# A two-layer graph network with pre-norm on one core: where the last rounds' aggregates stand, who scales two norms, and the first batch of the W2 stage

## The chip, the cores and the metric

The kernel runs on one core of a Trainium2 chip. Its time is the device time in microseconds (us) of one execution. The engines are PE (TensorE; PEld is its weight load), DVE (VectorE), ACT (ScalarE), POOL (GpSimd) and SP (SyncE, which here only issues DMAs); each runs its own queue in order, and semaphores join them.

## What is computed

The input is x (16 batches, 512 tokens, 128 features) and an adjacency matrix. Two residual blocks follow, each on relu(layernorm(x)).

```python
h = relu(layernorm(x)); x = x + L0(h, adj)
h = relu(layernorm(x)); x = x + L1(h, adj)

# L0: two graph layers, then LSTMs over windows of 1 to 4 tokens
h = relu(einsum('ts,bsh->bth', adj, x @ Wg0 + bg0))
h = relu(einsum('ts,bsh->bth', adj, h @ Wg1 + bg1))
for p in (1, 2, 3, 4):
    last = lstm_last(Wih[p-1], Whh[p-1], ..., windows of p tokens)
    h = h.at[:, last token of each window].set(last)

# L1: normalised adjacency, two linear layers, two batch norms over all tokens
A_hat = A_norm * dinv[:, None] * dinv[None, :]
agg = einsum('nm,bmd->bnd', A_hat, features)
h = relu(batchnorm(agg @ W1.T + b1, g1, be1))     # 256 features
out = batchnorm(h @ W2.T + b2, g2, be2)           # 128 features
```

A batch norm needs the statistics of all 16 batches, so it is a barrier between stages.

## The kernel before, in words

Every float32 product is made of three matmuls with operands split in a high and a low part (`product`, lines 1020 to 1022): ACT writes the high part (`..._hi`), DVE the low part (`..._lo`, `low`, lines 712 and 714).

The 16 batches go through the LSTM in four rounds of four batches, two chains of two batches each. A round has 22 turns (`ORDER`), 11 for each chain; the whole has 88 (`N_SLOTS`). In each turn every engine runs its `lstm_turn`. Behind a turn come pieces of other stages: `PRE_AFTER` and `POST_AFTER` are lists by turn, filled from the positions in `PRE_POS` and `POST_POS`. The pieces of L1 for a batch n below 12 (`LATE`) come one round after its LSTM: "turn" (PE transposes the batch's states, DVE adds them to x1, line 812), "stats" (DVE's statistics, lines 758 and 761), "norm" (POOL computes the layer norm: lines 347 and 348, the power at 350, four scalings of 128x128 at 353; then ACT's nrm_hi, line 571, and DVE's nrm_lo), "agg" (12 matmuls of 512 columns into post_ps; ACT's agg_hi, line 597; DVE's agg_lo) and "hid0" and "hid1" (W1, three matmuls each; ACT writes z, line 592; DVE takes its statistics, line 820). For batch 11 the aggregate stands behind turn 85, W1's halves behind 86 and 87, which are the last two turns. A position is the place in each engine's queue; nothing is reordered at run time.

Behind the last turn each engine has its own hand-written list for batches 12 to 15. PE: four groups of transposes, alternately into pre_ps and post_ps, then aggregates and W1 halves, each aggregate one batch ahead of its W1. POOL: the four norms in order, into `y_last`. DVE and ACT: as PE's list needs them.

Then comes the first batch norm (`batch_norm`, DVE lines 962 to 974, POOL's power at 393). The W2 stage goes over the batches in `END_ORDER`, 8 to 11 first, the spilled 0 to 7, then 12 to 15. For the k-th of them, z's two halves of 128x512 are scaled and shifted in place; who does it is fixed by `DVE_HALVES` (line 988), `ACT_HALVES` (679) and `POOL_HALVES`, which are all others (406). Then ACT makes hid_hi (693, both halves at once, 128x1024), DVE hid_lo (712), PE the six matmuls of W2, ACT takes them out (671) and DVE takes the statistics (993). The second batch norm is built by the same functions, and the last stage scales (703, 414), transposes (1238), adds x1 (1012) and stores.

SP loads z_back back from memory once the graph layers of all batches are done, and x1_back (3 MB) once the LSTM is.

## Time and profile before

| | |
|---|---|
| median of 3 runs | 585.74 us |
| lowest and highest | 584.45 and 585.82 us |
| the profiled execution, its own time | 586.14 us |
| its span | 584.3 us |
| busy: PE, DVE, ACT, POOL | 517.1, 426.0, 358.1, 203.1 us |
| last LSTM turns and their moved pieces | 485.0 to 494.9 us |
| transposes, norms, aggregates and W1 of batches 12 to 15 | 494.9 to 524.6 us |
| first batch norm | 524.6 to 527.3 us |
| W2 stage | 527.3 to 566.3 us |
| second batch norm and last stage | 566.3 to 584.3 us |

Times in views are us from the start of the span. A timeline row gives start, duration, engine, line, operation, output<-input and forms; in brackets it has the idle time of the engine before it and the instruction that ended it. A duration is longer than the time to the next start where instructions overlap in the engine's pipeline. PEclk is TensorE's granted clock as a share of full speed.

### The profile page before, as it was taken

What the parts mean: (1) busy time and instruction counts of PE and PEld (TensorE: products, weight loads), DVE (VectorE), ACT (ScalarE), POOL (GpSimd) and SP (SyncE); (2) the same over time, 40 slices, a digit from 0 to 9 for tenths busy, and PEclk for the clock granted to TensorE, in tenths of its full rate; (3) what the DMA queues carried; (4) which work ended last, traced back from release to release, by engine and by line L of the source; (5) the groups of instructions that cost most, each with busy time, mean ns of one, the idle gap of its engine ahead of it and who ended that gap; (6) DMA issues with size and microseconds to landing.
All of it is one profiled execution on the core that took longest, in us unless ns stands there. A gap on an engine that the chain in (4) does not pass through costs nothing.

```text
span 584.3 us, 8178 instructions
## 1 busy us (share of the span) xinstructions
PE 517.1 (88%) x2769; PEld 443.8 (76%) x2769; DVE 426.0 (73%) x968; ACT 358.1 (61%) x680; POOL 203.1 (35%) x310
## 2 busy tenths in 40 slices
PE   4998998798899999999999999998699989685856
PEld 3787687798887789899877898997487978464536
DVE  3656757878867888687688886856767876666876
ACT  2545755556468567575776675756647766157854
POOL 5402021304400854163008442510233241709941
PEclk9999999798999999999999999999989989796998
DMA  8300020000001111010110210105510000500007
GB/s 232 94 19 2 0 91 19 2 17 2 19 18 56 37 72 52 22 48 27 54 74 19 72 55 1 55 2 186 211 36 1 20 18 2 216 0 1 1 0 289
DMA packets 17838, 31.22 MB, mean 53 GB/s; under 512 B 1498, under 2 KB 6020, under 8 KB 17796
## 3 DMA queue, kind: packets, MB, share of 16 engines
q1 hardware_dynamic: 16804, 30.17, 14.9%
q10 hardware_dynamic: 992, 0.52, 0.4%
q8 instruction: 22, 0.36, 0.3%
q14 instruction: 20, 0.16, 0.1%
HBM read 19.16 MB, written 11.53 MB: 53 GB/s over the span
## 4 chain that ended last, share of the span: by engine, by line
PE 50%; issue 18%; DVE 13%; POOL 9%; ACT 6%; POOLq 2%; DMA 1%; DVEq 0%; ACTq 0%
PE gate_ps L1020 10%; PE gate_ps L1021 10%; PE gate_ps L1022 10%; POOL z_back L406 4%; PE pre_ps L1021 4%; PE pre_ps L1022 4%; PE pre_ps L1020 4%; PE post_ps L1020 2%; POOL x_pre L353 2%; PE post_ps L1022 2%; PE post_ps L1021 2%; ACT gate L626 2%; POOLq L351 2%; ACT gate L616 1%; DVE cell L894 1%
## 5 line engine op out<-in xcount | busy, mean ns | idle before, releaser
L616 ACT ACTIVATE gate<-gate_ps,gate_bias 128x256 f32<-128x256 f32 (+2 forms) x312 | 164.8, 564 | 48.0 <-PE gate_ps L1022 46.4
L1020 PE MATMUL gate_ps<-by_class_hi,wih_hi 128*128 128x256 f32 (+2 forms) x264 | 86.5, 328 | 12.5 <-POOL by_class_lo L372 6.8
L626 ACT ACTIVATE gate<-cell 128x512 f32<-128x512 f32 (+2 forms) x88 | 45.3, 515 | 69.1 <-DVE cell L889 35.7
L1022 PE MATMUL gate_ps<-by_class_lo,wih_hi 128*128 128x256 f32 (+2 forms) x264 | 84.9, 322 | 0.0
L1021 PE MATMUL gate_ps<-by_class_hi,wih_lo 128*128 128x256 f32 (+2 forms) x264 | 84.9, 321 | 0.0
L1020 PEld LDWEIGHTS gate_ps<-by_class_hi,wih_hi 128*128 128x128 f32 x264 | 51.2, 194 | 19.6 <-POOL by_class_lo L372 7.5
L1020 PE MATMUL gate_ps<-hstep_hi,whh_hi 128*128 128x256 f32 (+2 forms) x192 | 61.2, 319 | 0.0
L1021 PE MATMUL gate_ps<-hstep_hi,whh_lo 128*128 128x256 f32 (+2 forms) x192 | 61.2, 319 | 0.0
L1022 PE MATMUL gate_ps<-hstep_lo,whh_hi 128*128 128x256 f32 (+2 forms) x192 | 61.0, 318 | 0.0
L372 POOL TENSOR_TENSOR by_class_lo<-h,by_class_hi 128x256 fp32r<-128x256 f32 (+1 forms) x40 | 35.4, 891 | 61.0 <-ACT by_class_hi L624 61.0
L347 POOL TENSOR_TENSOR ln_pre<-mv_pre,eps 128x4 f32<-128x4 f32 x16 | 5.0, 316 | 143.0 <-DVE mv_pre L761 143.0
L1021 PEld LDWEIGHTS gate_ps<-by_class_hi,wih_lo 128*128 128x128 f32 x264 | 51.1, 193 | 3.7
L1022 PEld LDWEIGHTS gate_ps<-by_class_lo,wih_hi 128*128 128x128 f32 x264 | 51.0, 193 | 2.3
L347 POOL TENSOR_TENSOR ln_post<-mv_post,eps 128x4 f32<-128x4 f32 x16 | 6.1, 383 | 132.5 <-DVE mv_post L761 132.5
L899 DVE TENSOR_TENSOR gate<-gate 128x256 f32<-128x256 f32 (+2 forms) x48 | 26.8, 558 | 26.4 <-ACT gate L626 26.4
L1022 PEld LDWEIGHTS gate_ps<-hstep_lo,whh_hi 128*128 128x128 f32 x192 | 37.5, 195 | 1.4
L1021 PEld LDWEIGHTS gate_ps<-hstep_hi,whh_lo 128*128 128x128 f32 x192 | 37.5, 195 | 1.3
L1020 PEld LDWEIGHTS gate_ps<-hstep_hi,whh_hi 128*128 128x128 f32 x192 | 37.5, 195 | 1.3
L353 POOL TENSOR_SCALAR x_pre<-x_pre,ln_pre 128x128 f32<-128x128 f32 x64 | 34.8, 558 | 2.8 <-issue 2.8
L353 POOL TENSOR_SCALAR y_post<-x,ln_post 128x128 f32<-128x128 f32 x56 | 34.8, 636 | 2.5 <-issue 2.5
L886 DVE TENSOR_TENSOR gate<-gate 128x256 f32<-128x256 f32 (+2 forms) x48 | 24.2, 504 | 15.1 <-ACT gate L616 15.0
L889 DVE TENSOR_TENSOR cell<-cell,gate 128x256 f32<-128x256 f32 (+2 forms) x48 | 25.5, 532 | 5.0
(285 smaller groups left out, 1393.9 us busy)
## 6 DMA issues: line engine op xcount, KB each, us to landing
x_pre<-in_x SPq DMA_DIRECT2D x16, 256.0 KB, 2.7
x<-in_x SPq DMA_DIRECT2D x16, 256.0 KB, 2.7
z_spill<-z_ring SPq DMA_DIRECT2D x8, 512.0 KB, 2.8
z_back<-z_spill SPq DMA_DIRECT2D x8, 512.0 KB, 7.2
x_spill<-x SPq DMA_DIRECT2D x12, 256.0 KB, 2.2
x_back<-x_spill SPq DMA_DIRECT2D x1, 3072.0 KB, 11.1
out<-x_back SPq DMA_DIRECT2D x12, 256.0 KB, 2.3
x<-in_adj SPq DMA_DIRECT2D x1, 1024.0 KB, 6.3
```

The source lines that it names most:

```text
L351: nc.gpsimd.drain()
L353: last = nc.gpsimd.tensor_scalar(y[:, c * P:(c + 1) * P], src[:, c * P:(c + 1) * P], ln[:, 2, c:c + 1], ln[:, 1, c:c + 1], ALU.add, ALU.mult)
L372: nc.gpsimd.tensor_tensor(lo, states, f32(hi), ALU.subtract).then_inc(later_lo, 1)
L406: nc.gpsimd.tensor_scalar(zz, zz, bn1[:, 4, half:half + 1], bn1[:, 5, half:half + 1], ALU.mult, ALU.add).then_inc(t_pool, 1)
L616: nc.scalar.activation(gate[:, tile_of(g), gt, 0:size], gate_ps[k % GATE_BANKS][:, 0:size], ACT.Tanh if gt == G_GATE else ACT.Sigmoid, bia ...
L626: nc.scalar.activation(gate[:, tile_of(g), G_GATE, 0:size], cell[:, tile_of(g), 0:size], ACT.Tanh)\
L886: nc.vector.tensor_tensor(i_, i_, g_, ALU.mult).then_inc(ig_done, 1)
L889: nc.vector.tensor_tensor(c_, c_, i_, ALU.add).then_inc(cell_ready, 1)
L899: nc.vector.tensor_tensor(i_, o_, g_, ALU.mult).then_inc(h_done, 1)
L1020: nc.tensor.matmul(ps, w[0], m[0], start=start, stop=False)
L1021: nc.tensor.matmul(ps, w[1], m[0], start=False, stop=False)
L1022: return nc.tensor.matmul(ps, w[0], m[1], start=False, stop=stop)
```

## The change

Four things change.

The aggregate and W1 of batch 11 (`LEFT`) leave `POST_AFTER`. They now stand in the hand-written lists: the aggregate between the second and third group of transposes, W1 behind the fourth. The tables `TURN_PS`, `AGG_PS` and `HID_PS` say which PSUM bank each group of transposes, aggregate and W1 half uses, and the lists are written out anew.

For batches 12 and 13 POOL computes only the norm's scale (`norm_scale`), and DVE does the four scalings (`tail_y_of`); batches 14 and 15 stay with POOL.

In `batch_norm` DVE negates the mean while POOL computes the power, and the last two dependent instructions become one for each group.

In the W2 stage DVE scales both halves of the first batch, and ACT scales half (1, 1) in place of (0, 1), so POOL has 24 halves in place of 25. For the first batch hid_hi and hid_lo are made half by half, and PE starts with the first half.

```diff
--- before.py
+++ after.py
@@ -89,8 +89,8 @@
-DVE_HALVES = ((0, 0),)
-ACT_HALVES = ((0, 1), (3, 1), (5, 1), (8, 1), (11, 1), (14, 1))
+DVE_HALVES = ((0, 0), (0, 1))
+ACT_HALVES = ((1, 1), (3, 1), (5, 1), (8, 1), (11, 1), (14, 1))
 POOL_HALVES = tuple((k, half) for k in range(BATCHES) for half in range(HALVES)
@@ -114,8 +114,9 @@
               if len(ORDER) * (n // PER_ROUND - 1) + spots[n % PER_ROUND] == slot] for slot in range(N_SLOTS)]
+LEFT = LATE - 1
 POST_AFTER = [[(kind, n) for kind, spots in POST_POS.items() for n in range(LATE)
-               if len(ORDER) * (n // PER_ROUND + 1) + spots[n % PER_ROUND] == slot] for slot in range(N_SLOTS)]
+               if (n < LEFT or kind in ("turn", "stats", "norm")) and len(ORDER) * (n // PER_ROUND + 1) + spots[n % PER_ROUND] == slot] for slot in range(N_SLOTS)]
@@ -199,7 +200,7 @@
         cell = sb("cell", [P, CHAINS, T], F32, main)
-        y_last = [y_post, cell[:, 0, :]]
+        y_last = [y_post[:, :], cell[:, 0, :]]
         main.close()
@@ -224,6 +225,11 @@
         post_ps = whole.enter_context(nc.psum_tensor("post_ps", [P, T], F32))
+        TURN_PS = {LATE: pre_ps, LATE + 1: post_ps, LATE + 2: gate_ps[1], LATE + 3: gate_ps[2]}
+        AGG_PS = {LEFT: gate_ps[0], LATE: gate_ps[5], LATE + 1: pre_ps, LATE + 2: post_ps, LATE + 3: gate_ps[5]}
+        HID_PS = {LEFT: (gate_ps[3], gate_ps[4]), LATE: (gate_ps[0], gate_ps[1]), LATE + 1: (gate_ps[2], gate_ps[3]),
+                  LATE + 2: (gate_ps[4], pre_ps), LATE + 3: (gate_ps[0], gate_ps[1])}
@@ -254,6 +260,7 @@
         turn_mm, x1_ready = sem("turn_mm"), sem("x1_ready")
+        tail_rstd, tail_y = sem("tail_rstd"), sem("tail_y")
         post_stats, post_y, post_nhi, post_nlo = (sem(f"post_{n}") for n in ("stats", "y", "nhi", "nlo"))
@@ -340,14 +347,18 @@
-            def layer_norm(n, y, src, mv, ln, stats, ready):
+            def norm_scale(n, mv, ln, stats):
...
                 nc.gpsimd.drain()
-                nc.gpsimd.tensor_tensor(ln[:, 1, :], ln[:, 0, :], minus_half[:, :], ALU.pow)
+                return nc.gpsimd.tensor_tensor(ln[:, 1, :], ln[:, 0, :], minus_half[:, :], ALU.pow)
+            def layer_norm(n, y, src, mv, ln, stats, ready):
+                norm_scale(n, mv, ln, stats)
                 nc.gpsimd.drain()
@@ -386,7 +397,9 @@
-            for n in range(LATE, BATCHES):
+            for n in range(LATE, LATE + 2):
+                norm_scale(n, mv_post[n % 2], ln_post[n % 2], post_stats).then_inc(tail_rstd, 1)
+            for n in range(LATE + 2, BATCHES):
                 norm_post(n, y_last[n % 2])
@@ -566,8 +579,8 @@
-            def normed(n, y, dst, ready, done):
-                act.wait_ge(ready, n + 1)
+            def normed(n, y, dst, ready, done, count=None):
+                act.wait_ge(ready, n + 1 if count is None else count)
                 nc.scalar.activation(dst[0][:, :, :].rearrange("p c d -> p (c d)"), y, ACT.Relu).then_inc(done, 1)
@@ -655,16 +668,30 @@
-            for n in range(LATE, LATE + 2):
-                normed(n, y_last[n % 2][:, :], nrm[n % 2], post_y, post_nhi)
-            for n in range(LATE, BATCHES + 1):
-                if n < BATCHES:
-                    agg_out(n, gate_ps[n % 2], n % 2)
-                if n + 2 < BATCHES:
-                    normed(n + 2, y_last[n % 2][:, :], nrm[n % 2], post_y, post_nhi)
-                if n > LATE:
-                    for half in range(HALVES):
-                        hid_out(n - 1, half, gate_ps[2 + 2 * ((n - 1) % 2) + half])
+            def tail_norm(n):
+                if n < LATE + 2:
+                    normed(n, y_last[n % 2], nrm[n % 2], tail_y, post_nhi, n - LATE + 1)
+                else:
+                    normed(n, y_last[n % 2], nrm[n % 2], post_y, post_nhi, n - 1)
+            def tail_hid(n):
+                for half in range(HALVES):
+                    hid_out(n, half, HID_PS[n][half])
+            agg_out(LEFT, AGG_PS[LEFT], 1)
+            tail_norm(LATE)
+            tail_hid(LEFT)
+            tail_norm(LATE + 1)
+            agg_out(LATE, AGG_PS[LATE], 0)
+            tail_norm(LATE + 2)
+            agg_out(LATE + 1, AGG_PS[LATE + 1], 1)
+            tail_hid(LATE)
+            tail_norm(LATE + 3)
+            agg_out(LATE + 2, AGG_PS[LATE + 2], 0)
+            tail_hid(LATE + 1)
+            agg_out(LATE + 3, AGG_PS[LATE + 3], 1)
+            tail_hid(LATE + 2)
+            tail_hid(LATE + 3)
@@ -682,12 +709,17 @@
                 for j, half in ACT_HALVES:
-                    if j == (k + 1 if k else 0):
+                    if j == k + 1:
                         hid_t(j, half)
-                act.wait_ge(t_dve, halves_to(DVE_HALVES, k))
+                if k == 0:
+                    for half in range(HALVES):
+                        act.wait_ge(t_dve, half + 1)
+                        nc.scalar.activation(hid[0][0][:, half, :], z_end(b)[:, half * T:(half + 1) * T], ACT.Relu)\
+                            .then_inc(hid_hi, 1)
+                    continue
                 act.wait_ge(t_act, halves_to(ACT_HALVES, k))
-                if k > 0:
-                    act.wait_ge(t_pool, halves_to(POOL_HALVES, k))
+                act.wait_ge(t_pool, halves_to(POOL_HALVES, k))
                 if k >= 3:
@@ -943,21 +975,46 @@
-            for n in range(LATE, BATCHES):
-                turned(n, (pre_ps, post_ps)[n % 2])
-                if n < LATE + 2:
-                    stats_post(n)
-            for n in range(LATE, LATE + 2):
-                normed(n, y_last[n % 2][:, :], nrm[n % 2], post_nhi, post_nlo)
-                stats_post(n + 2)
-            for n in range(LATE, BATCHES + 1):
-                if n < BATCHES:
-                    agg_out(n, gate_ps[n % 2], n % 2)
-                if n + 2 < BATCHES:
-                    normed(n + 2, y_last[n % 2][:, :], nrm[n % 2], post_nhi, post_nlo)
-                if n > LATE:
-                    for half in range(HALVES):
-                        hid_stats(n - 1, half)
+            def tail_y_of(n):
+                dve.wait_ge(tail_rstd, n - LATE + 1)
+                for c in range(CHUNKS):
+                    last = nc.vector.tensor_scalar(y_last[n % 2][:, c * P:(c + 1) * P],
+                                                   x1[:, n % PER_ROUND, c * P:(c + 1) * P], ln_post[n % 2][:, 2, c:c + 1],
+                                                   ln_post[n % 2][:, 1, c:c + 1], ALU.add, ALU.mult)
+                last.then_inc(tail_y, 1)
+            def tail_norm(n):
+                normed(n, y_last[n % 2], nrm[n % 2], post_nhi, post_nlo)
+            def tail_hid(n):
+                for half in range(HALVES):
+                    hid_stats(n, half)
+            turned(LATE, TURN_PS[LATE])
+            stats_post(LATE)
+            turned(LATE + 1, TURN_PS[LATE + 1])
+            stats_post(LATE + 1)
+            agg_out(LEFT, AGG_PS[LEFT], 1)
+            tail_y_of(LATE)
+            turned(LATE + 2, TURN_PS[LATE + 2])
+            tail_norm(LATE)
+            tail_y_of(LATE + 1)
+            stats_post(LATE + 2)
+            tail_norm(LATE + 1)
+            turned(LATE + 3, TURN_PS[LATE + 3])
+            stats_post(LATE + 3)
+            agg_out(LATE, AGG_PS[LATE], 0)
+            tail_norm(LATE + 2)
+            agg_out(LATE + 1, AGG_PS[LATE + 1], 1)
+            tail_hid(LEFT)
+            tail_norm(LATE + 3)
+            tail_hid(LATE)
+            agg_out(LATE + 2, AGG_PS[LATE + 2], 0)
+            tail_hid(LATE + 1)
+            agg_out(LATE + 3, AGG_PS[LATE + 3], 1)
+            tail_hid(LATE + 2)
+            tail_hid(LATE + 3)
@@ -966,12 +1023,16 @@
                 nc.vector.tensor_scalar(bn[:, 2, :], bn[:, 1, :], EPS, None, ALU.add).then_inc(var, 1)
+                nc.vector.tensor_scalar(bn[:, 0, :], bn[:, 0, :], -1.0, None, ALU.mult).then_inc(part, 1)
                 dve.wait_ge(rstd, 1)
                 nc.vector.tensor_tensor(bn[:, 4, :], bn[:, 3, :], gamma, ALU.mult).then_inc(scale, 1)
+                dve.wait_ge(part, 1)
                 dve.wait_ge(scale, 1)
-                nc.vector.tensor_tensor(bn[:, 5, :], bn[:, 0, :], bn[:, 4, :], ALU.mult).then_inc(part, 1)
-                dve.wait_ge(part, 1)
-                nc.vector.tensor_tensor(bn[:, 5, :], beta, bn[:, 5, :], ALU.subtract).then_inc(ready, 1)
+                for a in range(len(groups)):
+                    last = nc.vector.scalar_tensor_tensor(out=bn[:, 5, a:a + 1], in0=bn[:, 0, a:a + 1],
+                                                          scalar=bn[:, 4, a:a + 1], in1=beta[:, a:a + 1],
+                                                          op0=ALU.mult, op1=ALU.add)
+                last.then_inc(ready, 1)
@@ -995,7 +1056,14 @@
             for k, b in enumerate(END_ORDER):
-                dve.wait_ge(hid_hi, k + 1)
+                if k == 0:
+                    for half in range(HALVES):
+                        dve.wait_ge(hid_hi, half + 1)
+                        hi, lo = (part[:, half, :] for part in hid[0])
+                        low(lo, z_end(b)[:, half * T:(half + 1) * T], hi, relu=True).then_inc(hid_lo, 1)
+                    continue
+                dve.wait_ge(hid_hi, k + 2)
                 hi, lo = (part[:, :, :].rearrange("p a t -> p (a t)") for part in hid[k % 3])
@@ -1196,33 +1264,44 @@
-            for n in range(LATE, BATCHES):
-                if n == LATE:
-                    pe.wait_ge(pre_lo, 4 * BATCHES)
-                elif n == LATE + 1:
-                    pe.wait_ge(z_ready, 2 * LATE)
-                else:
-                    pe.wait_ge(x1_ready, n - 1)
-                turn(n, (pre_ps, post_ps)[n % 2])
-            pe.wait_ge(gates_act, N_GATES)
-            agg_mms(LATE, gate_ps[0], 0)
-            for n in range(LATE, BATCHES):
-                if n + 1 < BATCHES:
-                    if n > LATE:
-                        pe.wait_ge(agg_lo, n)
-                    agg_mms(n + 1, gate_ps[(n + 1) % 2], (n + 1) % 2)
+            def tail_hid(n):
                 pe.wait_ge(agg_lo, n + 1)
                 for half in range(HALVES):
-                    if n >= LATE + 2:
-                        pe.wait_ge(z_ready, 2 * n + half - 3)
-                    hid_mms(half, gate_ps[2 + 2 * (n % 2) + half], n % 2)
+                    hid_mms(half, HID_PS[n][half], n % 2)
+            pe.wait_ge(pre_lo, 4 * BATCHES)
+            turn(LATE, TURN_PS[LATE])
+            pe.wait_ge(z_ready, 2 * LEFT)
+            turn(LATE + 1, TURN_PS[LATE + 1])
+            pe.wait_ge(gates_act, N_GATES)
+            agg_mms(LEFT, AGG_PS[LEFT], 1)
+            turn(LATE + 2, TURN_PS[LATE + 2])
+            turn(LATE + 3, TURN_PS[LATE + 3])
+            tail_hid(LEFT)
+            agg_mms(LATE, AGG_PS[LATE], 0)
+            pe.wait_ge(x1_ready, LATE + 1)
+            agg_mms(LATE + 1, AGG_PS[LATE + 1], 1)
+            pe.wait_ge(x1_ready, LATE + 3)
+            tail_hid(LATE)
+            agg_mms(LATE + 2, AGG_PS[LATE + 2], 0)
+            pe.wait_ge(x1_ready, LATE + 4)
+            pe.wait_ge(z_ready, 2 * LEFT + 1)
+            tail_hid(LATE + 1)
+            agg_mms(LATE + 3, AGG_PS[LATE + 3], 1)
+            pe.wait_ge(z_ready, 2 * LEFT + 2)
+            tail_hid(LATE + 2)
+            pe.wait_ge(z_ready, 2 * LATE + 2)
+            tail_hid(LATE + 3)
...
             for k in range(BATCHES):
-                pe.wait_ge(hid_lo, k + 1)
+                if k > 0:
+                    pe.wait_ge(hid_lo, k + 2)
                 if k >= GATE_BANKS:
...
                 for half in range(HALVES):
+                    if k == 0:
+                        pe.wait_ge(hid_lo, half + 1)
                     last = product(gate_ps[k % GATE_BANKS][:, :], [part[:, half, :] for part in w2],
...
```

## Rows read from the trace of the kernel before

**Rows 1.** The page, part 1: busy us (share of the span) and instructions.

```profile
PE 517.1 (88%) x2769; PEld 443.8 (76%) x2769; DVE 426.0 (73%) x968; ACT 358.1 (61%) x680; POOL 203.1 (35%) x310
```

**Rows 2.** Windows: us, busy PE, PEld, DVE, ACT, POOL, then PEclk, DMA, GB/s.

```profile
485.04:494.94 9.90, 9.90 (x69) 9.14 (x67) 6.24 (x16) 6.53 (x14) 0.73 (x1) 1.00 0.00 0
494.94:503.90 8.96, 2.74 (x18) 2.01 (x16) 7.04 (x26) 1.62 (x3) 4.41 (x10) 0.88 0.68 252
503.90:523.20 19.30, 19.25 (x72) 14.96 (x72) 10.90 (x29) 8.79 (x14) 8.00 (x18) 0.88 0.12 46
...
531.10:564.70 33.60, 27.84 (x96) 18.63 (x96) 27.17 (x30) 25.73 (x33) 29.18 (x22) 0.93 0.00 1
```

**Rows 3.** The timeline of PE, 485 to 523 us: start us, us, instruction.

```profile
485.04 0.40 PE L1020 MATMUL post_ps<-hat_hi,nrm_hi 128*128 128x512 f32 x1
...
487.79 0.28 PE L1020 MATMUL gate_ps<-by_class_hi,wih_hi 128*128 128x256 f32 x1
...
494.23 0.40 PE L1020 MATMUL post_ps<-agg_hi,w_hi 128*128 128x512 f32 x1
...
494.94 0.60 PE L1105 MATMUL pre_ps<-ident,h 128*128 128x128 f32 x4
...
503.90 0.76 PE L1020 MATMUL gate_ps<-hat_hi,nrm_hi 128*128 128x512 f32 x1 [3.68 <-DVE nrm_lo L712]
...
508.67 0.40 PE L1022 MATMUL gate_ps<-hat_lo,nrm_hi 128*128 128x512 f32 x1
...
521.50 0.50 PE L1020 MATMUL gate_ps<-agg_hi,w_hi 128*128 128x512 f32 x1
```

**Rows 4.** The timeline of DVE, 487 to 525 us.

```profile
487.52 0.42 DVE L714 TENSOR_TENSOR hstep_lo<-gate,hstep_hi 128x256 fp32r<-128x256 f32 x1
...
495.66 0.43 DVE L916 TENSOR_TENSOR h<-gate 128x256 f32<-128x256 f32 x1 [0.48 <-ACT gate L626]
...
496.84 0.67 DVE L812 TENSOR_TENSOR x<-pre_ps,x 128x512 f32<-128x512 f32 x1
...
498.79 0.66 DVE L812 TENSOR_TENSOR x<-post_ps,x 128x512 f32<-128x512 f32 x1
...
523.92 0.69 DVE L820 BATCH_NORM_STATS2 stats<-z_back 128x6 f32<-128x512 f32 x1
```

**Rows 5.** The timeline of POOL, the norm of batch 12.

```profile
500.63 1.74 POOL L353 TENSOR_SCALAR y_post<-x,ln_post 128x128 f32<-128x128 f32 x4 [0.17 <-issue]
```

**Rows 6.** The chain of waits, where POOL hands over: start us, us, what.

```profile
555.33 1.74 POOL z_back L406
```

**Rows 7.** The groups by line of DVE, each form apart: its two scalings.

```profile
L854 DVE TENSOR_SCALAR z_ring<-ident,dinv 128x128 f32<-128x128 f32 x4 | 0.9, 281 | 2.2 <-POOL dinv L387 2.2
...
L988 DVE TENSOR_SCALAR z_ring<-z_ring,bn 128x512 f32<-128x512 f32 x1 | 0.5, 547 | 0.0
```

**Rows 8.** The timeline of DVE, the first batch norm.

```profile
526.70 0.16 DVE L970 TENSOR_TENSOR bn<-bn,vec 128x2 f32<-128x2 f32 x1 [0.81 <-POOL bn L393]
...
526.90 0.16 DVE L972 TENSOR_TENSOR bn<-bn 128x2 f32<-128x2 f32 x1
```

**Rows 9.** The instructions of line L406 on POOL: duration ns min/median/max.

```profile
L406 POOL TENSOR_SCALAR z_back<-z_back,bn x20: 766/1734/1836, 533.4 to 558.5; 128x512 f32<-128x512 f32 x20
```

**Rows 10.** The timelines of POOL and DVE in the W2 stage.

```profile
527.36 1.03 POOL L406 TENSOR_SCALAR z_ring<-z_ring,bn 128x512 f32<-128x512 f32 x1 [0.69 <-DVE bn L974]
...
540.70 1.20 DVE L712 SCALAR_TENSOR_TENSOR hid_lo<-z_back,hid_hi 128x1024 fp32r<-128x1024 f32 x1
...
540.81 1.75 POOL L406 TENSOR_SCALAR z_back<-z_back,bn 128x512 f32<-128x512 f32 x1
```

**Rows 11.** The timeline of PE, a start, and two windows.

```profile
477.70 0.45 PE L1020 MATMUL gate_ps<-by_class_hi,wih_hi 128*128 128x256 f32 x1 [1.92 <-POOL by_class_lo L372]
...
500.00:501.00 1.00, 0.22 (x2) 0.03 (x1) 0.93 (x7) 0.00 (x0) 0.83 (x2) 1.00 1.03 403
501.00:502.00 1.00, 0.00 (x0) 0.00 (x0) 0.98 (x2) 0.00 (x0) 1.00 (x4) 0.88 0.98 375
```

## The prediction, made before the change was run

> **What bounds the kernel now.** First the busy shares of the engines: PE is busy for 88% of the span [rows 1], so the time is mostly TensorE's. That is an average, so the next view is the table by stage. In the last two turns of the LSTM PE has no idle time at all; in the 8.96 us after them it works 2.74 us; then come 19.30 us of aggregates and W1 in which it is full again; in the W2 stage it has gaps [rows 2]. The change touches just these four stretches.
>
> The PE timeline shows what fills the first [rows 3]. The aggregate of batch 11 starts at 485.04 and the next turn's first matmul at 487.79: 2.75 us for its twelve 512-column matmuls. Its W1 half 0 stands one turn later, and half 1 behind the last LSTM matmul, from 494.23 to the first transposes at 494.94, 0.70 us for three matmuls. Then the four groups of transposes trickle, each held by post_ps or pre_ps being read, and the first aggregate of the last round starts only at 503.90, behind 3.68 us of idling. DVE's timeline tells who made it late [rows 4]: the state of the last turn is written at 495.66, x of batch 12 at 496.84, POOL's norm takes the time to 502.37 (its four scalings start at 500.63 and last 1.74 us [rows 5]), and ACT's nrm_hi and DVE's nrm_lo follow before PE is released.
>
> In the W2 stage the chain of waits runs through POOL. Its 25 half-batch transforms, L406, follow each other without idle time, and ACT's hid_hi of the fourteenth batch is released by the one of 555.33 + 1.74 = 557.07 [rows 6]. From there to the end of the stage it is DVE's and PE's remainder, the same before and after.
>
> **The LSTM's end.** Twelve plus three matmuls leave the path ahead of the last LSTM matmul: 2.75 + 0.70 = 3.45 us. PE may use this only as far as its operands are there. The second to last turn needs hstep_lo written by 485.04, which the row before it gave; the last one needs hstep_lo of 487.52 + 0.42 = 487.94 [rows 4], and PE would come to it at about 488.05. That is a margin of 0.1 us; I take 0.15 us off for starts. So the LSTM's matmuls end at 494.23 - 3.3 = 490.9, and the last state (495.66 + 0.43) is there at 492.8. POOL's by_class_lo for these turns doesn't depend on what is moved.
>
> **The stretch to the first aggregate of the last round.** On PE: eight transposes (0.60 us per four, by the group at 494.94 [rows 3]) end at 492.1, the aggregate of batch 11 takes 2.75 + 0.1 to 495.0, the other eight transposes end at 496.2. All of this is ahead of DVE, which is now the one that is late. DVE from 492.8: x and statistics of a batch take 498.79 - 496.84 = 1.95 us [rows 4], two of them to 496.7; agg_lo of batch 11 to 497.4, after which PE does its W1 halves (1.40 us); then the norm's scaling of batch 12, four 128x128 instructions. The nearest row for them is L854, the same operation and shape on DVE, 281 ns each and 0.9 us for four [rows 7]; POOL's rstd has come by then (its scalings could start at 500.63, 3.8 us behind x of batch 12 at 496.84; from 492.8 that is 496.6). The bounds are 0.55 us, one DVE scaling of 512 columns [rows 7], and POOL's 1.74 us. That gives 498.3; x of batch 14 (0.67 us, ACT's nrm_hi beside it) 498.95; nrm_lo, taken like x at 0.67, 499.65. Two waits are new here. Behind DVE's wait for rstd stand x of batch 14 and all later statistics, and behind PE's wait for agg_lo of batch 11 stands the aggregate of batch 12; neither costs more than is counted, since rstd comes first and nrm_lo comes later. PE starts the aggregate of batch 12 at 499.8 in place of 503.90: **4.1 us earlier**. Against the naive view, the 4.15 us of work that were moved are not the gain; the gain is what DVE's queue lets through.
>
> **The aggregates and W1.** From 499.8 PE has the seven blocks before the last W1: 4 x 2.75 + 3 x 1.40 = 15.2 us, with starts 15.6. Next in line, nrm_lo of batch 13 is ready at 502.3 and PE wants it at 502.65; that of batch 14, still on POOL's long path (3.4 us from the statistics at 501.7, then 1.4 us for ACT and DVE) at 506.6, and PE wants it at 506.85. Both margins are 0.3 us, so whatever is slower than I say shows at once. agg_hi, agg_lo and the statistics of z fall between. The last W1 starts at 515.4, where before it was 521.50 [rows 3]. The blocks took 521.50 - 503.90 = 17.6 us before, because the eleven matmuls up to 508.67 took 4.77 us, 0.43 each, at the low clock (the granted clock of this stage is 0.88 in the mean [rows 2], between the levels 0.50, 1.2 GHz, and 1.00, 2.4 GHz) in place of eleven times 0.23: 2.2 us. In the new order I let the clock stay at 1.00, so that part, **about 2.0 us**, is gained too; its condition is the first rival. From the last W1 to the end of the last statistics it stays 524.61 - 521.50 = 3.1 us [rows 3, 4]. Sum of the tail: 6.1 us.
>
> **The batch norms.** The row pair 526.70 and 526.90 shows a step of 0.20 us between dependent tiny instructions [rows 8]. One step goes (the negation of the mean lies in the 0.81 us that DVE waits for POOL's pow); for bn1 a second, independent instruction is added at about 0.1 us, half of a dependent step. Gain 0.1 at bn1 and 0.2 at bn2, **0.3 us**; no row shows this instruction with a pointer operand at this size, so it may as well be 0 or a loss of 0.1.
>
> **The W2 stage.** POOL prepares 24 halves in place of 25, DVE two in place of one; ACT keeps six, its first now being (1, 1). An L406 takes 1.32 us on average, and that would be the saving. But its rows have two values, 0.77 us and about 1.74 us [rows 9], and a long one lies beside a hid_lo of DVE: 1.75 us at 540.81 beside 1.20 us at 540.70 [rows 10]; twelve of the 25 are such pairs. Twenty-two POOL steps at 0.77 and thirteen hid_lo at 0.97 make 29.5 us of the 29.7 between 527.36 and 557.07: the two take turns, and neither's work is hidden by the other. Taking one POOL half away gives only 0.77 us. DVE's added half costs part of it: the first L406 lies beside DVE's scaling of 0.55 us and takes 1.03 in place of 0.77 [rows 7, 10], so 0.26 us goes back. **Gain 0.5 us**; bounds 1.3 (the average) and a loss of 0.3 (the whole 0.55 on the path, and hid_lo's split). The Trainium skill (SBUF — State Buffer, section Who interferes with whom) says that GpSimd and a DVE instruction with two SBUF inputs hold one shared port in turn, for the whole instruction; the trace agrees, 1.74 being 0.77 + 0.97. By the average instead of this rule the sum would be 0.8 us lower. Handing PE the first half-batch early gains nothing: PE has gaps later on and the POOL chain sets the end.
>
> The queues: SP's reload of x1_back waits for the LSTM's end and so starts 3.3 us earlier; it takes 11.1 us and is wanted at the last stage, so it costs nothing. POOL's queue loses 2 x 1.74 us ahead of the norm of batch 14, which waits for DVE's statistics anyway.
>
> **Sum.** 6.1 + 0.3 + 0.5 = 6.9 us, against the profiled execution's 586.14: 579.2. That execution is 0.40 above the median of the runs, so 578.8 by the median. About 0.3% (1.8 us) is what a measurement of this kernel can tell from no change.
>
> **Rivals.** *The clock falls after the last transposes* (20%). The rows allow it: behind a gap of 1.92 us the matmul at 477.70 takes 0.45 us for 256 columns [rows 11] against 0.28 at 487.79, and the granted clock fell between 501 and 502, where PE is idle [rows 11]; my order has gaps of 1.3 and 0.7 us between 496.2 and 499.8. Against it: the clock held 1.00 through 500 to 501 although PE had only transposes with pauses since 494.94 [rows 11], and it is 0.93 over the W2 stage, where PE idles 5.8 of 33.6 us [rows 2]. Price: one spell as before, 2.1 us, so 580.9. The Trainium skill (TensorE: Matmul & The Clock Gate, section Part 4: PE-mode transpose) says that the full clock does not engage for transposes; by it the fall would be the rule here, while the trace shows 1.00 over four groups of them.
>
> *The LSTM's end doesn't move* (8%): the last turns wait for each other's states, not for PE. For it: the margin of 0.1 us. Against it: PE without idle time. It costs the 3.3 us: 582.1. *DVE's scaling is as slow as POOL's* (5%): 0.85 us for each of two batches, 580.5. *The first two together* (4%) leave 1.5 us: 584.2, no change.
>
> *Slower* (3%): the clock keeps falling in the tail, because PE now meets its waits one by one instead of working off a backlog. Its place is 497.5 to 517, its price 0.20 us for each 512-column matmul (0.43 against 0.23), 78 of them; from 35 slow ones on the gain is gone, with all of them 594.2. Before, it was eleven.
>
> **Numbers.** The likeliest case has 60%, own range 577.6 to 580.2. The range goes down to 577.0 (W2's 1.3 and the cheap scaling, with 0.6 for the scatter of the runs) and up to 582.2, so that the first three rivals are in; with what each case scatters around its own number, about 2 in 10 stay outside. Faster by over 0.3%: 0.93; within 0.3%: 0.04; slower: 0.03.
>
> **What would show it.** The last LSTM matmul near 491; the first aggregate of batch 12 at about 499.8, released by nrm_lo; four DVE scalings of about 0.28 us each; PEclk 1.00 from 497 to 515; the last statistics at 518.5; L406 x24, about half of them long, ending 0.5 us earlier counted from bn1. It is wrong if PE waits inside the last LSTM turns, if the clock is 0.50 behind 497, or if PE waits over 0.5 us for nrm_lo of batches 13 to 15.

## The result and the profile after

| | before | after |
|---|---|---|
| median of 6 runs each | 585.62 us | 577.00 us |
| lowest and highest | 582.82 and 585.94 us | 575.99 and 578.64 us |
| the profiled execution, its own time | 586.14 us | 577.82 us |
| its span | 584.3 us | 576.0 us |

The medians lie 8.6 us apart. The ratio is 0.9869 with a 95% interval of 0.985 to 0.9888; by it the change is worth 7.7 us, give or take 1.1. Predicted were 578.8 us and a range of 577.0 to 582.2; the median is at the low end of that range.

The page, part 1, of after (busy us, share of the span, instructions) answers to [rows 1]:

```profile
PE 513.6 (89%) x2769; PEld 440.0 (76%) x2769; DVE 428.6 (74%) x979; ACT 357.9 (62%) x681; POOL 199.4 (35%) x301
```

PE has the same 2769 instructions and 3.5 us less busy time: part of the gain is matmuls that ran at the full clock instead of half of it. The windows of after (us, busy PE, PEld, DVE, ACT, POOL, then PEclk, DMA share, GB/s) answer to [rows 2]:

```profile
477.00:487.90 10.90, 10.90 (x82) 10.77 (x81) 7.55 (x19) 7.31 (x18) 1.46 (x2) 0.88 0.02 5
487.90:497.95 10.05, 7.63 (x47) 6.33 (x46) 8.58 (x31) 3.96 (x9) 2.83 (x6) 1.00 0.58 191
497.95:515.84 17.89, 17.57 (x72) 13.20 (x72) 13.38 (x36) 9.16 (x16) 6.50 (x14) 1.00 0.19 70
523.50:560.00 36.50, 27.15 (x94) 17.36 (x93) 29.25 (x36) 27.04 (x35) 29.22 (x23) 0.95 0.00 1
```

The second and third line are the stretch to the first aggregate of the last round and the aggregates and W1. Before, the granted clock was 0.88 in both [rows 2]; now it is 1.00 in both. The timeline of PE in after (start, duration, instruction, in brackets idle time and what ended it) answers to [rows 3]:

```profile
489.04 0.28 PE L1090 MATMUL gate_ps<-hstep_lo,whh_hi 128*128 128x256 f32 x1
489.16 0.62 PE L1173 MATMUL pre_ps<-ident,h 128*128 128x128 f32 x4
489.62 0.61 PE L1173 MATMUL post_ps<-ident,h 128*128 128x128 f32 x4
489.99 0.47 PE L1088 MATMUL gate_ps<-hat_hi,nrm_hi 128*128 128x512 f32 x1
...
492.82 1.04 PE L1173 MATMUL gate_ps<-ident,h 128*128 128x128 f32 x8
495.54 0.50 PE L1088 MATMUL gate_ps<-agg_hi,w_hi 128*128 128x512 f32 x1 [1.67 <-DVE agg_lo L746]
...
497.95 0.50 PE L1088 MATMUL gate_ps<-hat_hi,nrm_hi 128*128 128x512 f32 x1 [0.75 <-DVE nrm_lo L744]
...
505.44 0.50 PE L1088 MATMUL post_ps<-hat_hi,nrm_hi 128*128 128x512 f32 x1 [0.16 <-DVE nrm_lo L744]
...
514.15 0.47 PE L1088 MATMUL gate_ps<-agg_hi,w_hi 128*128 128x512 f32 x1
```

The last LSTM matmul stands at 489.04. Transposes, batch 11's aggregate and its W1 follow, with two gaps, and batch 12's aggregate begins at 497.95. Then PE goes through to the last W1 half pair at 514.15 with one wait of 0.16 us. The timeline of DVE shows what released these:

```profile
490.58 0.43 DVE L948 TENSOR_TENSOR h<-gate 128x256 f32<-128x256 f32 x1 [0.48 <-ACT gate L639]
490.93 0.68 DVE L844 TENSOR_TENSOR x<-pre_ps,x 128x512 f32<-128x512 f32 x1
...
494.82 0.66 DVE L746 TENSOR_TENSOR agg_lo<-gate_ps,agg_hi 128x512 fp32r<-128x512 f32 x1
495.40 1.11 DVE L982 TENSOR_SCALAR y_post<-x,ln_post 128x128 f32<-128x128 f32 x4
496.42 0.68 DVE L844 TENSOR_TENSOR x<-gate_ps,x 128x512 f32<-128x512 f32 x1
497.20 0.69 DVE L744 SCALAR_TENSOR_TENSOR nrm_lo<-y_post,nrm_hi 128x512 fp32r<-128x512 f32 x1
...
515.84 1.39 DVE L852 BATCH_NORM_STATS2 stats<-z_back 128x6 f32<-128x512 f32 x2 [0.35 <-ACT z_back L605]
```

Between 490.58 and the start of nrm_lo at 497.20 DVE has no wait of more than 0.1 us: it is the engine that sets the start of batch 12's aggregate, as the prediction had it.

**Where the time went.** The two profiles are 8.3 us apart. To split that, each profile is cut at the same events. The first is the matmul behind the 1.9 us gap [rows 11], called the anchor: 477.70 before, 475.84 after. Nothing that was changed stands ahead of it. The tail is the stretch from the first matmul of batch 12's aggregate to the first batch norm.

| stretch, us | before | after | gain | predicted |
|---|---|---|---|---|
| start to anchor | 477.70 | 475.84 | 1.86 | 0 |
| anchor to the last LSTM state written | 18.39 | 15.17 | 3.22 | 3.3 |
| to the first matmul of batch 12's aggregate | 7.81 | 6.94 | 0.87 | 0.8 |
| to the first batch norm | 20.75 | 19.32 | 1.43 | 2.0 |
| first batch norm, to POOL's first transform | 2.71 | 2.79 | -0.08 | 0.1 |
| W2 stage, to the second batch norm | 38.94 | 38.13 | 0.81 | 0.5 |
| second batch norm, to POOL's first transform | 2.09 | 2.04 | 0.05 | 0.2 |
| last stage | 15.91 | 15.77 | 0.14 | 0 |
| behind the anchor | 106.60 | 100.16 | 6.44 | 6.9 |

So 6.4 us come from the places that the change touches; 1.9 us lie ahead of them and need another explanation.

### The profile page after: what moved, and what is told of

Read it like the earlier page. It is cut to its first block, busy times and chain, and to the rows that moved or that the text cites. A ratio compares the mean times of both kernels' runs of the same rounds, so it can differ in the third digit from the quotient of the medians.

```text
span 576.0 us, 8165 instructions
## 1 busy us (share of the span) xinstructions
PE 513.6 (89%) x2769; PEld 440.0 (76%) x2769; DVE 428.6 (74%) x979; ACT 357.9 (62%) x681; POOL 199.4 (35%) x301
## 4 chain that ended last, share of the span: by engine, by line
PE 49%; issue 18%; DVE 14%; POOL 10%; ACT 6%; POOLq 2%; DMA 1%; DVEq 0%; ACTq 0%
PE gate_ps L1088 10%; PE gate_ps L1090 9%; PE gate_ps L1089 9%; PE pre_ps L1089 4%; PE pre_ps L1090 4%; POOL z_back L419 4%; PE pre_ps L1088 4%; PE post_ps L1088 3%; PE post_ps L1090 2%; POOL x_pre L364 2%; PE post_ps L1089 2%; ACT gate L639 2%; POOLq L362 2%; ACT gate L629 1%; DVE cell L926 1%
## 5 line engine op out<-in xcount | busy, mean ns | idle before, releaser
L364 POOL TENSOR_SCALAR y_post<-x,ln_post 128x128 f32<-128x128 f32 x52 | 33.0, 647 | 2.3 <-issue 2.3
```

The source lines that it names most:

```text
L364: last = nc.gpsimd.tensor_scalar(y[:, c * P:(c + 1) * P], src[:, c * P:(c + 1) * P], ln[:, 2, c:c + 1], ln[:, 1, c:c + 1], ALU.add, ALU.mult)
```

## The experiments

All comparisons are with the kernel before, run on the same chip in the same series. Ratios have 95% intervals.

### Is it the move? e1_not_moved

The kernel after, but with batch 11's aggregate and W1 back in the LSTM's last turns:

```diff
-               if (n < LEFT or kind in ("turn", "stats", "norm")) and len(ORDER) * (n // PER_ROUND + 1) + spots[n % PER_ROUND] == slot] for slot in range(N_SLOTS)]
+               if len(ORDER) * (n // PER_ROUND + 1) + spots[n % PER_ROUND] == slot] for slot in range(N_SLOTS)]
...
-            pe.wait_ge(z_ready, 2 * LEFT)
+            pe.wait_ge(z_ready, 2 * LATE)
-            agg_mms(LEFT, AGG_PS[LEFT], 1)
-            tail_hid(LEFT)
```

> The changed kernel with one part undone: aggregate and W1 of batch 11 stand behind turns 85 to 87 of the LSTM again, the rest of the new lists stays. If the move is what lets DVE and PE start the tail early, the last LSTM state comes 3.2 to 3.3 us later, DVE then saves the 0.6 us of agg_lo, so the aggregate of batch 12 starts about 2.7 us later than in the changed kernel, PE idles 4 to 5 us in front of it and its clock falls, which costs 2.2 more: 577.0 + 2.7 to 4.9 = 579.7 to 581.9. If the moved work was only displaced (it takes the same place in a queue that is full anyway), 577 to 578.

Measured: 585.16 us against 584.45, ratio 0.9997 (0.9978 to 1.0017). By the runs the whole gain is gone: 585.16 is 8.2 us above the 577.0 of after, where 2.7 to 4.9 were expected. Its timeline of PE shows where:

```profile
502.62 0.80 PE L1084 MATMUL gate_ps<-hat_hi,nrm_hi 128*128 128x512 f32 x1 [5.42 <-DVE nrm_lo L742]
503.21 0.63 PE L1085 MATMUL gate_ps<-hat_hi,nrm_lo 128*128 128x512 f32 x1
503.64 0.63 PE L1086 MATMUL gate_ps<-hat_lo,nrm_hi 128*128 128x512 f32 x1
...
508.33 0.42 PE L1085 MATMUL pre_ps<-hat_hi,nrm_lo 128*128 128x512 f32 x1
508.59 0.40 PE L1086 MATMUL pre_ps<-hat_lo,nrm_hi 128*128 128x512 f32 x1
```

PE idles for 5.42 us where after it has work, and behind that the matmuls stand 0.43 us apart up to 508.33, then 0.23. That is the slow spell of before, back again: from batch 12's aggregate to the batch norm it takes 21.36 us against 19.32 in after. Behind the anchor this kernel takes 104.9 us; before_again (below), whose LSTM end also ran at the full clock, takes 105.4. After takes 100.2, and 1.5 of these are a slow spell behind the anchor that e1_not_moved doesn't have (below), so 98.7 is to be compared. So everything but the move is worth about 0.5 us, and the move itself some 6 us: 3.2 from the LSTM's end and 2.0 from the clock, with the rest spread over the other stretches. The expectation fell short for two reasons: from the anchor to batch 12's aggregate it is 3.5 us more than with the move (24.1 against the 20.6 of e4, e5 and e8, all three without that spell), not 2.7; and the anchor itself stands at 478.52 in this profile, 2.7 us later than in after, although nothing ahead of it differs.

### Does the clock need the work, or only something to do? e7_filled

The kernel before, with 14 matmuls that feed nothing put ahead of batch 12's aggregate:

```diff
+            for _ in range(14):
+                nc.tensor.matmul(gate_ps[5][:, :], w1[0][:, 0, :], hat[0][:, 0, :], start=True, stop=True)
```

> The kernel before, with 14 extra matmuls of 512 columns into the idle bank gate_ps[5], issued behind the last transposes where PE idled 3.68 us; their result is never read. It measures the clock's part alone. If the slow matmuls after the gap come from the idling, the spell of eleven matmuls at 0.43 us vanishes, the time from the aggregate of batch 12 to the last statistics goes from 20.75 to 18.7, and the time from 585.6 to 583.5, though nothing is computed earlier. If the clock follows something else, the spell stays and the time is 585.6, or up to 0.5 more because the extra matmuls delay the aggregate.

Measured: 583.82 us against 584.87, ratio 0.9983 (0.9962 to 1.0004): no change. The timeline of PE and two windows of this kernel:

```profile
499.40 5.93 PE L1209 MATMUL gate_ps<-hat_hi,w_hi 128*128 128x512 f32 x14
505.16 0.40 PE L1020 MATMUL gate_ps<-hat_hi,nrm_hi 128*128 128x512 f32 x1
```

```profile
500.00:505.00 5.00, 5.00 (x14) 3.88 (x13) 2.96 (x11) 0.75 (x2) 4.68 (x13) 0.53 1.04 392
505.16:524.00 18.84, 16.99 (x73) 13.26 (x71) 11.61 (x24) 9.19 (x15) 5.84 (x12) 1.00 0.01 3
```

The filler did not hold the clock up; the clock had fallen before it could (0.50 from 498 to 499, ahead of the filler's start at 499.40, and 0.53 over 500 to 505), and the filler itself took 5.93 us, 0.42 each. It paid for the spell: the real aggregate began 2.2 us late (9.96 us behind the last state against 7.81) and everything behind it ran at 1.00 and took 18.50 us against 20.75. That puts the price of a spell at about 2.2 us, and makes it zero-sum to pay it with idle matmuls in this place. That a filler placed earlier would keep the clock up was not shown.

### The norms: e2_pool_norms, e9_split_norms

Norms of batches 12 and 13 given back to POOL:

```diff
-            for n in range(LATE, LATE + 2):
-                norm_scale(n, mv_post[n % 2], ln_post[n % 2], post_stats).then_inc(tail_rstd, 1)
-            for n in range(LATE + 2, BATCHES):
+            for n in range(LATE, BATCHES):
...
-            tail_y_of(LATE)
...
-            tail_y_of(LATE + 1)
```

> The changed kernel with POOL doing the whole norm of batches 12 and 13 again. In the changed kernel's trace the statistics of batch 12 are there at 492.97 and DVE's scalings end at 496.51; POOL's path needs 3.4 us from the statistics, so it would have y at 496.4, the same. For batch 13 POOL would be about 0.9 us later, for 14 about 0.8 earlier. If so, DVE's norms are worth nothing: 576.7 to 577.4, the aggregate of batch 12 within 0.2 us of its place. If DVE's norms are what starts the tail early, the aggregate of batch 12 starts 1 to 2 us later and the time is 578 to 579.

Measured: 577.4 us against 584.45, ratio 0.9871 (0.9835 to 0.9906). The distance from the last LSTM state to batch 12's aggregate is 6.88 us, against 6.94. Giving the scalings to DVE is worth nothing: POOL's are slower (1.74 us [rows 5] against 1.11), but lie beside DVE's other work.

That suggests sharing them. POOL takes blocks 2 and 3, DVE blocks 0 and 1:

```diff
+                nc.gpsimd.drain()
+                for c in range(2, CHUNKS):
+                    last = nc.gpsimd.tensor_scalar(y_last[n % 2][:, c * P:(c + 1) * P],
...
+                last.then_inc(post_y, 1)
...
-                for c in range(CHUNKS):
+                for c in range(2):
```

> In the tail, the norms of batches 12 and 13 are divided: POOL scales blocks 2 and 3 of each, DVE blocks 0 and 1; the rest is as after. Theory 1 (the norm of batch 12 is on the path only as the last thing before its aggregate, a few tenths): DVE's own part falls from 1.11 us (four scalings) to about 0.55, and POOL's two lie beside it, so the first matmul of batch 12's aggregate comes 0.3 to 0.6 us earlier behind the last LSTM state (6.4 to 6.6 instead of 6.94) and the kernel is 0.3 to 0.6 us faster than after: 576.4 to 576.7 against 577.0. Theory 2 (the two engines disturb each other in SBUF, as POOL and DVE do at the feed-forward transforms, and a second semaphore must be met): nothing is gained, 576.8 to 577.3, and the distance stays at 6.9 to 7.0.

Measured: 576.73 us against 583.47, ratio 0.9897 (0.9852 to 0.9942); after_again stood at 577.71 in the same series. One of its four runs stands at 582.27, 5 us above the highest of the others, and no trace tells why. The interval is too wide for half a microsecond, but the timeline of PE has it:

```profile
495.30 0.50 PE L1093 MATMUL gate_ps<-agg_hi,w_hi 128*128 128x512 f32 x1 [1.68 <-DVE agg_lo L751]
497.20 0.50 PE L1093 MATMUL gate_ps<-hat_hi,nrm_hi 128*128 128x512 f32 x1 [0.24 <-DVE nrm_lo L749]
```

PE's wait for nrm_lo is 0.24 us where it was 0.75, and the distance is 6.42 us in place of 6.94. Theory 1 holds for the place of the aggregate; that the kernel as a whole is faster by it, the runs can't tell.

### The batch norms: e3_old_bn

```diff
-                for a in range(len(groups)):
-                    last = nc.vector.scalar_tensor_tensor(out=bn[:, 5, a:a + 1], in0=bn[:, 0, a:a + 1],
...
+                nc.vector.tensor_tensor(bn[:, 5, :], bn[:, 0, :], bn[:, 4, :], ALU.mult).then_inc(part, 1)
+                dve.wait_ge(part, 1)
+                nc.vector.tensor_tensor(bn[:, 5, :], beta, bn[:, 5, :], ALU.subtract).then_inc(ready, 1)
```

> The changed kernel with batch_norm as before (two dependent instructions in place of one with a pointer operand for each group). From the last statistics to the first transform it took 2.62 us before and takes 2.72 now at the first norm, 2.02 and 1.97 at the second. So this run has 2.6 and 2.0 again and a time that is the same, 576.9 to 577.0. Forecast theory: 0.3 us slower.

Measured: 578.12 us against 584.45, ratio 0.9883 (0.9849 to 0.9917). The stretches are 2.71 us at the first batch norm and 2.10 at the second, as in before; after has 2.79 and 2.04. The four runs, 577.0 to 579.2 us, can't show differences of this size. The timelines of DVE, first of after and then of e3_old_bn:

```profile
519.33 0.16 DVE L1028 TENSOR_TENSOR bn<-bn,vec 128x2 f32<-128x2 f32 x1 [0.75 <-POOL bn L406]
519.60 0.35 DVE L1032 SCALAR_TENSOR_TENSOR bn<-bn,vec 128x1 f32<-128x1 f32 x2
```

```profile
519.07 0.16 DVE L1027 TENSOR_TENSOR bn<-bn,vec 128x2 f32<-128x2 f32 x1 [0.81 <-POOL bn L406]
519.27 0.16 DVE L1029 TENSOR_TENSOR bn<-bn 128x2 f32<-128x2 f32 x1
519.46 0.16 DVE L1031 TENSOR_TENSOR bn<-vec,bn 128x2 f32<-128x2 f32 x1
```

The old way is ready at 519.62, 0.55 us behind its first row; the new at 519.95, 0.62 us behind. One dependent step fewer, but the step to the fused instruction is 0.27 us instead of 0.20, and a pair of them lasts 0.35.

### The W2 stage: e4, e5, e6, e8

e4_old_w2 gives the first batch back as it was, and hid_hi, hid_lo and W2 take both its halves at once again:

```diff
-DVE_HALVES = ((0, 0), (0, 1))
-ACT_HALVES = ((1, 1), (3, 1), (5, 1), (8, 1), (11, 1), (14, 1))
+DVE_HALVES = ((0, 0),)
+ACT_HALVES = ((0, 1), (3, 1), (5, 1), (8, 1), (11, 1), (14, 1))
```

> The changed kernel with the W2 stage as before (25 halves on POOL, DVE one, the first batch whole). The stage, from the first batch norm's end to the last statistics, took 39.0 us before and 38.2 now. Turn-taking theory: 39.0 again, 577.8. If the average price of a POOL half counted, the saving of 1.3 would show as 39.5.

Measured: 578.7 us against 584.45, ratio 0.989 (0.9854 to 0.9927). The stage takes 38.82 us against 38.13: the edit is worth 0.7, and the average theory, which wanted 1.3, is out.

e5_act_seven moves one more half from POOL to ACT, with nothing else beside it:

```diff
-ACT_HALVES = ((1, 1), (3, 1), (5, 1), (8, 1), (11, 1), (14, 1))
+ACT_HALVES = ((1, 1), (3, 1), (5, 1), (8, 1), (9, 1), (11, 1), (14, 1))
```

> The changed kernel with one more half of the W2 stage, (9, 1), given from POOL to ACT; nothing is added to DVE. Turn-taking theory (a POOL half and a hid_lo never run at once, so a POOL half is worth its own 0.77 us): the stage from the first transform to the second batch norm's first instruction goes from 38.1 to 37.4, and the time from 577.0 to 576.3. Average theory (a POOL half is worth 1.3): 36.8. If ACT has become the bound: 38.1 or more.

Measured: 575.85 us against 584.87, ratio 0.9859 (0.9838 to 0.988). The stage takes 37.38 us, 0.75 less than after. That is the short duration of a POOL half, not the average of 1.32: the turn-taking account holds.

e6_lo_from_psum asks for the cause. The low parts from the second batch on read PSUM in place of z, so that DVE's instruction has one input from SBUF:

```diff
-                low(lo, z_end(b), hi, relu=True).then_inc(hid_lo, 1)
+                low(lo, pre_ps[:, :].unsqueeze(1).broadcast_to([P, HALVES, T]), hi, relu=True).then_inc(hid_lo, 1)
```

> The changed kernel, but from the second batch on hid_lo takes its first operand from pre_ps in PSUM in place of z in SBUF; so the low part is left without z and the output is not the reference's. Every instruction is as long as before in elements; only the number of SBUF inputs of DVE's instruction goes from two to one. If it is the two SBUF inputs that make POOL wait, all L419 from the second on take 0.77 us, POOL is through in about 19 us, and the stage is bound by DVE (16 x 1.7 us + 3) or ACT: 31 to 33 us in place of 38.1, a time near 571. If POOL is slow for another reason, the rows at 1.74 stay and the stage takes 38.

Measured: 576.4 us in its one run; the stage takes 33.92 us. The groups by line, first of after, then of e6_lo_from_psum (busy us, mean ns | idle before):

```profile
L419 POOL TENSOR_SCALAR z_back<-z_back,bn 128x512 f32<-128x512 f32 x20 | 26.7, 1352 | 0.0
L744 DVE SCALAR_TENSOR_TENSOR hid_lo<-z_back,hid_hi 128x1024 fp32r<-128x1024 f32 x12 | 15.3, 1278 | 4.0 <-ACT hid_hi L725 4.0
```

```profile
L419 POOL TENSOR_SCALAR z_back<-z_back,bn 128x512 f32<-128x512 f32 x20 | 15.1, 775 | 0.0
L744 DVE SCALAR_TENSOR_TENSOR hid_lo<-pre_ps,hid_hi 128x1024 fp32r<-128x1024 f32 x15 | 18.2, 1215 | 3.0 <-ACT hid_hi L725 2.8
```

The same twenty halves fall from 1352 to 775 ns each, and none is long any more, while DVE's instruction stays about as long as it was (1278 and 1215 ns). So what these twenty waited for is DVE's second SBUF input. The stage gained 4.2 us where POOL's rows gained 11.6: ACT is now busy for 14.9 of the 15.0 us from 530 to 545, and DVE for 13.4; this is why 31 to 33 us was not reached. The time of this one run, 576.4 us, is far from the 571 expected, because its anchor stands at 478.29, 2.45 us later than in after (more on that below); behind the anchor it takes 96.3 us against 100.2. The rule of the Trainium skill (SBUF — State Buffer, section Who interferes with whom), that a DVE instruction with at most one SBUF input, outside the modes that use two ports, does not contend with GpSimd, agrees with the 775 ns.

e8_w2_spread uses that account: three more halves to DVE, one more to ACT, 20 left to POOL.

```diff
-DVE_HALVES = ((0, 0), (0, 1))
-ACT_HALVES = ((1, 1), (3, 1), (5, 1), (8, 1), (11, 1), (14, 1))
+DVE_HALVES = ((0, 0), (0, 1), (4, 0), (7, 0), (11, 0))
+ACT_HALVES = ((1, 1), (2, 1), (5, 1), (7, 1), (8, 1), (10, 1), (15, 1))
```

> The changed kernel with the halves of the W2 stage spread anew: DVE takes (4, 0), (7, 0) and (11, 0) too, ACT takes half 1 of batches 1, 2, 5, 7, 8, 10 and 15, POOL keeps 20. Turn-taking theory: four POOL halves go at 0.77 us, DVE's three added ones hold the shared path for some 0.3 us each, so 38.1 - 3.1 + 0.9 = 35.9 to 36.3 us for the stage and 574.9 to 575.2 in time. If DVE's own time is the bound by then (16 hid_lo at 1.13, 16 statistics at 0.60, five scalings at 0.5, with waits), the stage stays above 37.

Measured: 576.55 us against 584.87, ratio 0.9866 (0.9841 to 0.9892). The stage takes 36.84 us, 1.3 less than after, but 0.5 more than expected, and little below e5's 37.38 with one moved half. Its group of POOL says why:

```profile
L419 POOL TENSOR_SCALAR z_back<-z_back,bn 128x512 f32<-128x512 f32 x16 | 25.0, 1576 | 0.0
```

Four halves fewer save 1.7 us of the 26.7, not four times 0.77: the rest got longer in the mean, 1576 against 1352 ns. Beside two of DVE's three added scalings POOL's halves took 2.06 and 2.20 us, where 1.74 was the long value, and beside the third and two hid_lo 3.04, where before had 2.79 beside two hid_lo, so a half on DVE beside POOL's is not free, although the scaling has only one tensor as its input. At the first batch of after the two meet in the same way: POOL's first half takes 1.04 us and not 0.77, and DVE's second scaling 0.92 and not the 0.55 of its first. In which mode DVE's scalings run, no run shows.

### Both together, and the two kernels again: e10_both, after_again, before_again

e10_both has the edits of e8 and e9.

> The two edits together: the W2 stage's transforms spread over DVE, ACT and POOL as in the run before (W2 stage 36.84 us there against 38.13 after, 576.55 us), and the norms of batches 12 and 13 divided between POOL and DVE. If both costs are separate, the sum: 0.45 us below the 576.55 of the spreading alone if the division gains what theory 1 of it says, 576.1 in the middle; if the division gains nothing, 576.5. Either is 0.5 to 0.9 us below after and 8 to 9.5 below before.

> The kernel after, unaltered, for what differs from one execution to the next. If 1.9 us of the profiled pair's difference is luck at the start (slow-clock matmuls after 12 us, 10 in before's profile and none in after's) and not the change, then the median against before stays at 7.0 to 8.0 us, and of further executions of after some show those slow matmuls too, with the anchor (the matmul behind the gap at 475.84) at about 477.7 instead of 475.8. If the change itself removed them, no execution of after shows any, and the anchor stays at 475.8.

> The kernel before, unaltered, for a second profiled execution. Behind the anchor (the matmul that ends the gap near 477.70) it should repeat the first profile: 18.39 us to the last LSTM state, or 16.9 where no slow-clock matmuls follow that gap; 7.8 to batch 12's aggregate, 20.75 for the tail with its slow-clock spell, 106.6 or 105.1 us from the anchor to the end. If the slow-clock matmuls at 12 to 17 us are luck, they can be missing here, and the anchor is then near 475.8; if the kernel before always has them (they were in its profile and in those of both kernels with the unmoved work, three of three, and in four of ten with the moved work), they are here again and the anchor is at 477.5 to 478.5. Its time against the other executions of before: a ratio of 1.000 with an interval of 0.003 to both sides.

Measured, the first two in one series against 583.47 us of before: e10_both 576.1 us, ratio 0.9859 (0.9835 to 0.9883); after_again 577.71 us, ratio 0.9892 (0.987 to 0.9914). before_again: 584.9 us, ratio 0.9996 (0.9981 to 1.0012) against its own kind. The intervals of e10_both and after_again overlap, so their runs alone don't separate them. The stretches do: batch 12's aggregate 0.52 us earlier, the tail 0.2 and the W2 stage 1.3 shorter, 2.0 us in all, each where its edit is. So by the runs it beats before, and by the stretches of one profile after too.

The stretches of the repeats, in the profiles (us):

| | anchor | to last LSTM state | to aggregate 12 | tail | W2 stage | behind the anchor |
|---|---|---|---|---|---|---|
| before | 477.70 | 18.39 | 7.81 | 20.75 | 38.94 | 106.60 |
| before_again | 478.36 | 16.91 | 7.80 | 20.93 | 38.90 | 105.44 |
| after | 475.84 | 15.17 | 6.94 | 19.32 | 38.13 | 100.16 |
| after_again | 475.63 | 15.22 | 6.94 | 19.28 | 38.11 | 100.27 |
| e2_pool_norms | 477.46 | 13.67 | 6.88 | 19.36 | 38.11 | 98.94 |
| e10_both | 475.48 | 13.67 | 6.42 | 19.10 | 36.77 | 96.62 |

The stretch to the last state has two values, 1.5 us apart, for either order of the work: 18.39 and 16.91, 15.2 and 13.67. The difference between the orders is 3.2 us at either. Which value it is depends on the execution: before and before_again are the same kernel. The timelines of PE, first of before_again and then of after_again:

```profile
478.36 0.39 PE L1020 MATMUL gate_ps<-by_class_hi,wih_hi 128*128 128x256 f32 x1 [1.90 <-POOL by_class_lo L372]
478.58 0.28 PE L1021 MATMUL gate_ps<-by_class_hi,wih_lo 128*128 128x256 f32 x1
478.70 0.28 PE L1022 MATMUL gate_ps<-by_class_lo,wih_hi 128*128 128x256 f32 x1
```

```profile
475.63 0.39 PE L1088 MATMUL gate_ps<-by_class_hi,wih_hi 128*128 128x256 f32 x1 [1.92 <-POOL by_class_lo L383]
...
476.46 0.42 PE L1090 MATMUL gate_ps<-hstep_lo,whh_hi 128*128 128x256 f32 x1
476.67 0.41 PE L1088 MATMUL gate_ps<-by_class_hi,wih_hi 128*128 128x256 f32 x1
```

The same gap of 1.9 us is followed by a spell at half clock in one execution and by none in the other. An earlier place goes with it. The windows from 420 to 429 and from 474 to 483 us, first of before and then of before_again:

```profile
420.00:429.00 9.00, 6.67 (x22) 5.38 (x23) 6.76 (x17) 5.12 (x9) 5.75 (x8) 0.81 0.09 30
474.00:483.00 9.00, 7.08 (x44) 6.60 (x43) 6.73 (x15) 5.74 (x14) 4.40 (x7) 0.81 0.11 29
```

```profile
420.00:429.00 9.00, 6.21 (x28) 4.80 (x27) 7.39 (x21) 5.28 (x10) 5.12 (x7) 1.00 0.16 59
474.00:483.00 9.00, 7.10 (x56) 6.62 (x55) 7.20 (x17) 7.17 (x18) 5.62 (x8) 1.00 0.12 29
```

In all fourteen profiles the two windows go together: both have 0.81 in before, after, after_again, e3, e6 and e9, and both have 1.00 in the eight others. What decides it is not shown.

The spell in the tail is not like that. All four profiles with the unmoved work (before, before_again, e1, and e7, where it falls on the filler) have it; none of the ten with the moved work does: each of them has a granted clock of 1.00 in the window from 487 to 510 us, where before_again has 0.78.

Where in the unmoved tail the clock falls does differ. In before it fell behind 501 us, in the gap of 3.68 us, with all transposes done [rows 11], and in e1 in its long gap too. In before_again it fell at 498, and so it did in e7. The windows of before_again:

```profile
497.00:498.00 1.00, 0.47 (x4) 0.27 (x3) 0.93 (x9) 0.00 (x0) 0.00 (x0) 0.92 0.94 285
498.00:499.00 1.00, 0.31 (x2) 0.32 (x3) 0.96 (x4) 0.00 (x0) 0.72 (x3) 0.50 0.93 295
```

The fourth group of transposes, at 498.69, and the gap of 3.27 us come only after that. So the long gap is not needed for the fall; three groups of four transposes with pauses of 0.60 and 0.71 us, and the pause of 1.22 us that follows them, were enough in two of the four profiles.

There are places ahead of the anchor too. At 12 to 17 us 512-column matmuls come at 0.43 us each in some executions, some eight to eleven of them, which costs 1.5 to 2.1 us. Here the column of the granted clock doesn't tell: the window of before over these 6 us gives 1.00, with 15 matmuls, and that of after 1.00 with 24. It is in the profiles of before, before_again, e1 and e7, and in those of e2, e4, e5 and e8, but not in those of after, after_again, e3, e6, e9 and e10. That is four of four with the unmoved work and four of ten with the moved. The windows of before and of after:

```profile
12.00:18.00 6.00, 5.73 (x15) 4.55 (x16) 3.86 (x13) 1.09 (x2) 3.12 (x7) 1.00 0.49 130
```

```profile
12.00:18.00 6.00, 5.56 (x24) 4.53 (x25) 4.24 (x14) 2.75 (x8) 3.11 (x6) 1.00 0.41 116
```

The first matmul of that place in the timeline of PE, and what released it, in before_again and in after_again:

```profile
12.81 0.79 PE L1020 MATMUL pre_ps<-adj_t_hi,nrm_hi 128*128 128x512 f32 x1 [1.07 <-DVE nrm_lo L712]
```

```profile
12.27 0.50 PE L1088 MATMUL pre_ps<-adj_t_hi,nrm_hi 128*128 128x512 f32 x1 [0.88 <-DVE nrm_lo L744]
```

The idle time ahead of it is much the same; the durations are not. In the pair of before and after it makes up the 1.86 us: instruction by instruction on DVE, before is 0.2 us ahead of after at 12 us, 1.8 behind at 20 and 1.9 behind at the anchor. It is not the only place, as e6 shows, whose anchor stands at 478.29 without it. Its granted clock is 0.83 from 64 to 74 us, as in before_again, e1, e4, e7 and e8, and 1.00 in the eight others, before among them; that costs 1.5 us. The spell at 420 to 429 us costs 1.6, and between 100 and 160 us, where all fourteen have a slow spell of some length, up to 1.4 us are gained or lost. So the anchor stands anywhere from 475.5 to 478.5 us. That before has 1.00 at 64 to 74 us and before_again 0.83 shows chance at that place. At 12 us, that e2, e4, e5 and e8 have slow matmuls speaks for chance; that no kernel with the unmoved work is without them leaves open whether before has them more often. No run settles that. By the stretches behind the anchor the change is worth 6.4 us; by the two comparisons of runs 7.7 (ratio 0.9869) and 6.3 (0.9892).

## Why the prediction was right

**The LSTM's end: right.** Predicted 3.3 us, measured 3.2 in profiles with the spell behind the anchor and in those without. PE did not wait inside the last turns, so the second rival fell.

**The start of batch 12's aggregate: right.** 4.1 us earlier by the sum of this term and the last, measured 4.09. The parts were as told: no wait on DVE from the last state to nrm_lo, and 0.75 us of idle PE at its end. One part was sized low: the four scalings took 1.11 us, not 0.9. What the sum didn't say is that the scalings' place on DVE is worth nothing against POOL (e2). The third rival, a scaling as slow as POOL's, fell with the 1.11 us.

**The clock in the tail: right, and the largest thing at risk.** The first rival, with 20%, fell: in after PE idles 1.67 and 0.75 us in this stretch, and the granted clock is 1.00 all through, with transposes and batch 11's matmuls between the idle times. Before, with transposes alone and a gap of 3.68 us [rows 3], it fell. That the moved matmuls are what holds it up is the reading of ten profiles against four; the filler of e7 came too late to show it by itself, and whether it is their work or the shorter gaps that they leave is not separated. One argument against the rival was weaker than it looked: that the clock holds 1.00 over four groups of transposes with pauses was true of before, and of e1 with fewer pauses, while in before_again and e7 it fell among them, at 498. The rule that full clock does not engage for transposes (the Trainium skill, TensorE: Matmul & The Clock Gate, section Part 4: PE-mode transpose) is not contradicted by any of this: the clock was full before them, in before it held over all four groups, and in before_again it did not.

**The tail's blocks: mis-sized by 0.6 us.** The step was "4 x 2.75 + 3 x 1.40 = 15.2 us, with starts 15.6"; measured are 16.20, from 497.95 to 514.15, of which 0.16 is a wait for nrm_lo of batch 14. The prediction allowed 0.4 us for the starts of seven blocks. Only one aggregate (2.75) and one pair of W1 halves (1.40) kept to the size; the three others of the aggregates took 2.93, 2.84 and 2.89, their first matmul lasting 0.50 or 0.47 us rather than 0.40, and the two other pairs 1.72, wait and all, and 1.67. The margins for nrm_lo of batches 13 and 14, put at 0.3 us each, came out at nothing lost and 0.16 lost.

**The batch norms: wrong in size.** 0.3 us were predicted with the bound "0 or a loss of 0.1". Measured is a loss of 0.08 and a gain of 0.05, that is nothing. The step that failed is "a second, independent instruction is added at about 0.1 us": it takes 0.14 to 0.21, and the dependent step ahead of the fused one is 0.27 instead of 0.20.

**The W2 stage: right in its mechanism.** Predicted 0.5 us, measured 0.81, and 0.7 by e4. That a POOL half is worth its short duration was shown by e5 (0.75 us), and that the long ones wait for DVE's two-input instruction by e6. What DVE's second half costs was not measured apart. POOL's second half takes 1.44 us in place of 0.77, beside DVE's second scaling and first hid_lo, yet from the start of POOL's first half to the end of its last it is 32.12 us in place of 32.93, the whole 0.81; so the 0.26 us taken off did not show.

**The sum.** 6.9 us were predicted and 6.4 measured behind the anchor. The rest of the difference between the two profiles, 1.9 us, is a stretch of slow matmuls at the start that the prediction took to be the same in both. It may be why the median, 577.0, is lower than 578.8 although the local sum was too high; the other runs of that comparison have no trace, so this is not shown. The forecast does not need that luck: with the 6.4 us alone the time would be 585.7 - 6.4 = 579.3 us, inside the range.

## What to carry to other kernels

Work that can move from a full engine's critical stretch into its next idle stretch pays twice on TensorE: its own duration, as far as the operands allow, and the matmuls behind the idle stretch that no longer run at half clock (2.0 to 2.2 us here). Filler that arrives when the clock has already fallen pays nothing. Where POOL's rows of one operation come in two lengths, look for a DVE instruction with two SBUF inputs beside the long ones; taking one instruction from POOL is worth only the short length. And a difference of 1 or 2 us between two profiles must be cut at common events first, since four places of this kernel, at 12, 64, 420 and 474 us, run at either of two rates from one execution to the next.

## What was not expected of the hardware

- The same kernel, with the same gap of 1.9 us, goes on at the full clock in one execution and at half in another: 1.5 us each time. In fourteen profiles of fourteen it does what the place at 420 us did, some 50 us before.
- With transposes and pauses of 0.60 to 1.22 us alone, the clock held 1.00 through four groups in one execution of before and fell behind the third in the other.
- Matmuls of 512 columns at 0.43 us apart, over 12 to 17 us, under a granted clock that the profile gives as 1.00. What slows them is not known.
- With DVE's second operand in PSUM, POOL's 128x512 scaling takes 775 ns in the mean of 20, none over 791; beside a DVE instruction of much the same length with both operands in SBUF the mean is 1352 ns.
- Fused 128x1 instructions on DVE with a pointer scalar are dearer than plain 128x2 ones: 0.35 us for two, and a start 0.27 us behind the one they depend on.
- POOL's long halves, 1.74 us, took 2.06 and 2.20 us with a scaling of DVE's beside them as well (e8), although DVE's scaling reads only one tensor.
